# Routing in PSUM in a kernel of attention, mixture of experts, selective scan and mixing: one pair later, between two groups, with waits in another order

## The reference, cut to what matters

```python
h = _layernorm(x) * (1 + ca) + sa
x = x + ga * _L0_attn_ref(h, ...)        # 16 heads, grouped keys, relative positions
h = _layernorm(x) * (1 + cb) + sb
x = x + gb * _L0_ffn_ref(h, ...)         # mixture of 16 experts
...
x = x + ga * _L1_attn_ref(h, ...)        # selective scan, 256 channels x 16 states
x = x + gb * _L1_ffn_ref(h, ...)         # tanh of one product
```

```python
s = jax.nn.sigmoid(x2 @ Wg.T)
g = s.reshape(T, N_GROUPS, E // N_GROUPS)
_, gidx = jax.lax.top_k(g.max(axis=-1), TOPK_GROUPS)
group_mask = jnp.any(jax.nn.one_hot(gidx, N_GROUPS, dtype=jnp.bool_), axis=1)
masked = jnp.where(group_mask[:, :, None], g, -jnp.inf).reshape(T, E)
_, idx = jax.lax.top_k(masked, TOPK)
w = jnp.take_along_axis(s, idx, axis=1)
w = w / jnp.sum(w, axis=-1, keepdims=True) * ROUTE_SCALE
```

## Time and profile before

| | us |
|---|---|
| median of 3 runs | 2718.4 (2712.68 to 2719.95) |
| the profiled execution | 2723.16 |
| its span in the trace | 2721.4 |

### The profile page before, as it was taken

The page is one execution under the profiler, slowest core; times in us unless marked ns, Lnnn a source line. Parts: engine busy times, 40 slices in busy tenths (PEclk is TensorE's granted clock), DMA queues, the critical chain, the costliest instruction groups (busy, mean ns, idle before and its releaser), DMA issues.

```text
span 2721.4 us, 41804 instructions
## 1 busy us (share of the span) xinstructions
PE 2139.4 (79%) x11705; PEld 1002.0 (37%) x11840; DVE 1956.9 (72%) x3193; ACT 1624.3 (60%) x4159; POOL 1724.0 (63%) x2236
## 2 busy tenths in 40 slices
PE   4778988879798887878788887978888797877543
PEld 3344433434344333434343433434334343332110
DVE  2444658787786868777686868778587877778776
ACT  2655656666575666666566665757666566644442
POOL 1012258586776858577685857678585867777643
PEclk9889999999899999989899998989999899999665
DMA  7535395766667586665768676666857667454442
GB/s 141 90 61 102 58 177 109 148 129 143 122 112 156 104 158 127 147 125 117 136 120 166 121 133 126 127 130 124 164 109 146 127 140 129 97 127 128 118 117 69
DMA packets 534880, 338.84 MB, mean 125 GB/s; under 512 B 353929, under 2 KB 453177, under 8 KB 534201
## 3 DMA queue, kind: packets, MB, share of 16 engines
q1 hardware_dynamic: 534652, 336.16, 62.3%
HBM read 242.21 MB, written 26.74 MB: 99 GB/s over the span
## 4 chain that ended last, share of the span: by engine, by line
PE 30%; DVE 22%; POOL 16%; issue 14%; DMA 7%; ACT 7%; SPq 4%; POOLq 0%; ACTq 0%; DVEq 0%
DVE work L1241 6%; DMA bc<-bc_rows 5%; PE bank L623 5%; POOL work L1235 4%; POOL work L1248 4%; PE bank L909 3%; PE bank L954 3%; PE bank L651 3%; DVE nmax L631 3%; PE bank L1271 3%; POOL zh L967 2%; PE bank L972 2%; DVE step L1046 2%; PE bank L1072 2%; ACT probs L641 2%
## 5 line engine op out<-in xcount | busy, mean ns | idle before, releaser
L1235 POOL TENSOR_TENSOR work<-work,bc 128x512 f32<-128x512 f32 x512 | 658.5, 1292 | 188.7 <-PE bank L1271 132.7
L1241 DVE TENSOR_TENSOR_SCAN work<-bank,work 128x512 f32<-128x512 f32 x512 | 622.0, 1215 | 170.7 <-POOL work L1235 111.4
L1248 POOL TENSOR_TENSOR work<-work,bc 128x512 f32<-128x512 f32 x436 | 559.8, 1287 | 147.3 <-DVE work L1241 132.4
L967 POOL TENSOR_TENSOR zh<-zh,w_bc 128x512 f32<-128x512 f32 x256 | 326.9, 1277 | 403.4 <-DVE zh L960 403.1
L1224 ACT ACTIVATE bank<-work,neg_a 128x510 f32<-128x510 f32 x512 | 353.5, 691 | 370.1 <-DVE work L1241 349.5
L641 ACT ACTIVATE probs<-bank,nmax 128x256 f32<-128x256 f32 x1024 | 477.2, 479 | 69.2 <-DVE nmax L631 68.2
L631 DVE TENSOR_REDUCE nmax<-bank 128x2 f32<-128x512 f32 x512 | 336.0, 676 | 196.1 <-PE bank L623 195.9
L954 PE MATMUL bank<-h_b,w_t 128*128 128x512 f32 x512 | 293.7, 657 | 113.3 <-ACT probs L641 105.3
L651 PEld LDWEIGHTS bank<-ident,probs 128*128 128x128 f32 x2048 | 268.3, 151 | 293.8 <-issue 249.3
L659 ACT ACTIVATE probs_t<-bank 128x512 f32<-128x512 f32 x512 | 305.1, 596 | 106.6 <-PE bank L681 72.6
L623 PE MATMUL bank<-ke,q_all 64*64 64x256 f32 x4096 | 302.4, 413 | 84.4 <-DVE zh L960 47.8
(11 more groups left out here) (194 smaller groups left out, 2545.6 us busy)
## 6 DMA issues: line engine op xcount, KB each, us to landing
work<-dt_rows SPq DMA_DIRECT2D x256, 512.0 KB, 5.8
ke<-low SPq DMA_DIRECT2D x256, 256.0 KB, 5.8
w_bc<-w_rows_d SPq DMA_DIRECT2D x256, 256.0 KB, 5.1
q_all<-q_rows SPq DMA_DIRECT2D x1024, 8.0 KB
bc<-bc_rows SPq DMA_DIRECT2D x64, 256.0 KB, 8.4
x_in<-in_x SPq DMA_DIRECT2D x32, 256.0 KB, 5.5
dt_rows<-step SPq DMA_DIRECT2D x16, 512.0 KB, 3.5
dt_rows<-step SPq DMA_DIRECT2D x32, 256.0 KB, 2.5
```

Source lines behind the costliest of these rows:

```text
L967: nc.gpsimd.tensor_tensor(zh[:, n % 3, :], zh[:, n % 3, :], w_bc[:, n % WB, :], ALU.mult).then_inc(m_p, 1)
L1235: nc.gpsimd.tensor_tensor(hb[at % HB], ring[n % RING][:, 1, :], bc[:, s, :], ALU.mult).then_inc(s_dbx, 1)
L1241: nc.vector.tensor_tensor_scan(hb[at % HB], decay_bank(p, m)[:, :], hb[at % HB], 0.0, ALU.mult, ALU.add).then_inc(s_h, 1)
L1248: nc.gpsimd.tensor_tensor(hb[at % HB], hb[at % HB], bc[:, SG + batch(m)[2], :], ALU.mult).then_inc(s_hc, 1)
```

## The change

1. The results that the parts of the routing hand on lie in bank 3 of PSUM in turn with SBUF, so that no instruction has two inputs in SBUF. `route` cuts the bank. The group maximum is taken twice, into SBUF and into PSUM. The last two parts, times 0.5 * ROUTE_SCALE and times the score, become one; 20 parts are left.
2. They stand at steps 174 to 179 and not 167 to 178, behind the scaling of group 0 (step 173) of the next pair, for which part 0 waits (`groups_scaled`); the weights' transpose at 181 (178), its copy at 182 (179), the store at 183 (179), each expert's fetch one step earlier. The attention's statistics stand at -82 (-89), the last layernorm's at 512 (519). The last pair's routing keeps its steps but the last.
3. In seven functions the waits are listed in another order.

```diff
+        def route(lo, *shape):
+            ap = bank[3][:, lo:lo + math.prod(shape)]
...
-        equal = sb("equal", [P, TILES, NE])
-        top8 = sb("top8", [P, TILES, 8])
-        few = sb("few", [P, TILES])
-        ties = sb("ties", [P, TILES, NG, NG])
-        grank = sb("grank", [P, TILES, NG])
+        gate_p, ties_p, equal_p, picked_p = (route(64 * k, TILES, NE) for k in range(4))
+        ties = route(64, TILES, NG, NG)
+        gmax_p, open_p = (route(256 + 16 * k, TILES, NG) for k in range(2))
+        top8 = route(288, TILES, 8)
+        few = route(320, TILES)
...
-        ROUTE_STEPS, EXPERT, EVERY = 21, 192, 8
+        ROUTE_STEPS, EXPERT, EVERY = 20, 192, 8
...
-            68]], x_a_sync=-108, x_res_sync=104, a_store_sync=-33, m_store_sync=179,
-            m_fetch_sync=-8, s_rows_sync=376, s_rows_in_sync=[378, 391, 386, 380],
+            68]], x_a_sync=-108, x_res_sync=104, a_store_sync=-33, m_store_sync=183,
+            m_fetch_sync=-9, s_rows_sync=376, s_rows_in_sync=[378, 391, 386, 380],
...
-            m_route_vector=[167, 167, 167, 167, 169, 169, 169, 169, 170, 170, 170, 171, 172, 172,
-            173, 173, 174, 174, 174, 178, 178], m_end_vector=327, s_stats_vector=328,
+            m_route_vector=[174, 174, 174, 175, 175, 175, 175, 176, 176, 176, 177, 177, 177, 177, 178, 178, 178, 178, 179, 179], m_end_vector=327, s_stats_vector=328,
...
         def a_scores_tensor(pe, n, st):
             p, c = divmod(n, CHUNKS)
             b, x0 = c // (CHUNKS // 2), 2 * (c % (CHUNKS // 2))
+            if ups_before(st):
+                pe.wait_ge(m_b, ups_before(st))
+            if n:
+                pe.wait_ge(a_exp, n)
...
         def a_turn_tensor(pe, n):
-            pe.wait_ge(a_exp, n + 1)
             if n:
                 pe.wait_ge(a_tc, n)
+            pe.wait_ge(a_exp, n + 1)
...
         def a_turn_scalar(act, n):
-            act.wait_ge(a_t, n + 1)
             if n % CPG == 0 and n:
                 act.wait_ge(a_pv, n // CPG)
+            act.wait_ge(a_t, n + 1)
...
         def a_inverse_tensor(pe, n):
+            pe.wait_ge(a_ao, n + 1)
             pe.wait_ge(a_dg, n + 1)
-            pe.wait_ge(a_ao, n + 1)
...
-        def m_route_vector(dve, p, k):
+        def m_route_vector(dve, p, k, st):
             if k == 0:
                 dve.wait_ge(m_exp, p + 1)
+                if groups_scaled(st):
+                    dve.wait_ge(a_on, groups_scaled(st))
...
             elif k == 2:
-                nc.vector.tensor_reduce(gmax[:, :, :], score[:, :, :].rearrange("p t (g k) -> p t g k", g=NG), AX_X,
-                                        ALU.max).then_inc(m_ch, 1)
+                by_member = score[:, :, :].rearrange("p t (g k) -> p t g k", g=NG)
+                nc.vector.tensor_reduce(gmax[:, :, :], by_member, AX_X, ALU.max)
+                nc.vector.tensor_reduce(gmax_p, by_member, AX_X, ALU.max).then_inc(m_ch, 1)
             elif k == 3:
                 nc.vector.tensor_tensor(beats[:, :, :, :], other, own, ALU.is_gt)
-                nc.vector.tensor_tensor(ties[:, :, :, :], other, own, ALU.is_equal).then_inc(m_ch, 1)
+                nc.vector.tensor_tensor(ties, other, own, ALU.is_equal).then_inc(m_ch, 1)
...
             elif k == 15:
-                nc.vector.tensor_tensor(picked[:, :, :], picked[:, :, :], equal[:, :, :], ALU.add).then_inc(m_ch, 1)
+                nc.vector.tensor_tensor(picked_p, picked[:, :, :], equal_p, ALU.add).then_inc(m_ch, 1)
...
-            elif k == 19:
-                nc.vector.tensor_scalar(few[:, :], few[:, :], 0.5 * ROUTE_SCALE, None, ALU.mult).then_inc(m_ch, 1)
             else:
-                nc.vector.tensor_tensor(we[:, :, 0:NE], picked[:, :, :], few_e, ALU.mult).then_inc(m_ch, 1)
+                nc.vector.scalar_tensor_tensor(we[:, :, 0:NE], picked[:, :, :], 0.5 * ROUTE_SCALE, few_e, ALU.mult,
+                                               ALU.mult).then_inc(m_ch, 1)
...
         def m_gate_waits_tensor(pe, n):
 
+            if n:
+                pe.wait_ge(m_a, n)
...
-            act.wait_ge(s_in[n % RING], landed(p, n))
             if p >= FREE_PAIR and (p, m) != (FREE_PAIR, 0):
+                act.wait_ge(s_h, at - 1)
                 act.wait_ge(s_z1, 1)
-                act.wait_ge(s_h, at - 1)
             elif at:
                 act.wait_ge(s_h, at)
+            act.wait_ge(s_in[n % RING], landed(p, n))
...
         def s_input_gpsimd(pool, p, m):
             n, j, s = batch(m)
             at = BATCHES * p + m
+            if at >= HB:
+                pool.wait_ge(s_y, (at - HB) // 4 + 1)
+            pool.wait_ge(s_in[n % RING], landed(p, n))
             if m in (0, 4):
                 pool.wait_ge(bc_in[s], 16 * (p + 1))
```

More of the change, by code:

```diff
@@ L1 @@
 import itertools
+import math
 from contextlib import ExitStack
@@ L170, in build @@
         gz_t = [step[:, 2, :], step[:, 1, :]]
+        def route(lo, *shape):
+            ap = bank[3][:, lo:lo + math.prod(shape)]
+            if len(shape) == 1:
+                return ap
+            if len(shape) == 2:
+                return ap.rearrange("p (a b) -> p a b", b=shape[1])
+            return ap.rearrange("p (a b c) -> p a b c", b=shape[1], c=shape[2])
         gate = sb("gate", [P, TILES, NE])
@@ L444, in groups_valued, with groups_scaled @@
             return max(0, min(ALL_GROUPS, (st - 1 - AT["a_values_tensor"]) // GROUP_STEPS + 1))
+        def groups_scaled(st):
+            return max(0, min(ALL_GROUPS, (st - AT["a_scale_vector"]) // GROUP_STEPS + 1))
         def ln_stats_vector(dve, L, x, p):
@@ L787, in m_route_vector @@
             by_group = [P, TILES, NG, NG]
-            other, own = gmax[:, :, :].unsqueeze(2).broadcast_to(by_group), gmax[:, :, :].unsqueeze(3).broadcast_to(by_group)
+            other, own = gmax[:, :, :].unsqueeze(2).broadcast_to(by_group), gmax_p.unsqueeze(3).broadcast_to(by_group)
             flat_g, flat_e = "p t j i -> p t (j i)", "p t (g k) -> p (t g) k"
-            open_ = grank[:, :, :].rearrange("p t g -> p (t g)").unsqueeze(2).broadcast_to([P, TILES * NG, NE // NG])
+            open_ = open_p.rearrange("p t g -> p (t g)").unsqueeze(2).broadcast_to([P, TILES * NG, NE // NG])
@@ L791, in m_route_vector @@
             fourth = top8[:, :, TOPK - 1:TOPK].broadcast_to([P, TILES, NE])
[L792 removed]
+            few_e = few.unsqueeze(2).broadcast_to([P, TILES, NE])
             if k == 0:
[L795 removed]
+                nc.vector.tensor_scalar(gate_p, gate[:, :, :], 1.0, None, ALU.add).then_inc(m_ch, 1)
             elif k == 1:
[L797 removed]
+                nc.vector.reciprocal(score[:, :, :], gate_p).then_inc(m_ch, 1)
@@ L928, in m_gate_waits_tensor @@
                     pe.wait_ge(s_zg, 2 * ((n - GAP["z"][h]) // NE) + h + 1)
-            if n:
-                pe.wait_ge(m_a, n)
         def m_tanh_scalar(act, p, e):
@@ L1229, in s_input_gpsimd @@
             at = BATCHES * p + m
+            if at >= HB:
+                pool.wait_ge(s_y, (at - HB) // 4 + 1)
+            pool.wait_ge(s_in[n % RING], landed(p, n))
             if m in (0, 4):
                 pool.wait_ge(bc_in[s], 16 * (p + 1))
-            pool.wait_ge(s_in[n % RING], landed(p, n))
-            if at >= HB:
-                pool.wait_ge(s_y, (at - HB) // 4 + 1)
             nc.gpsimd.tensor_tensor(hb[at % HB], ring[n % RING][:, 1, :], bc[:, s, :], ALU.mult).then_inc(s_dbx, 1)
@@ L1623, in step_vector @@
                 if p is not None:
-                    m_route_vector(dve, p, k)
+                    m_route_vector(dve, p, k, st)
             p = due("m_end_vector", st)
```

47 lines of the change are left out of this document (20 added, 27 removed).

## The result

The median of five runs is 2692.7 us (2684.5 to 2703.1), beside 2717.8 us (2712.7 to 2720.0) for the kernel before: a ratio of 0.9913, 95% interval 0.9889 to 0.9938. That is 25 us off, where I forecast 43. Faster was right, the time lies in the range and 18 us above the forecast. The profiled execution has a span of 2694.6 us, against 2721.4.

The account below looks back on a forecast made before the run. VectorE's routing was taken to bound the stretch, its gain being how much earlier GpSimd gets on: 2.8 us x 13 pairs = 36, last pair 3, waits 4.5, together 43 off the median of 2718.4: 2675 us, range 2645 to 2711.

Parts of the forecast that it names:

- The stretched forms wait for GpSimd inside their own duration: VectorE's routing: nine long instructions wait on GpSimd over SBUF; PSUM operands shed 6.3 of 12.6 us a pair.
- VectorE's order set out anew: Routing stretch from 1036.8 us re-timed: root 1046.3, scan of step 52 ends 1056.7, GpSimd's instruction 1056.9 against 1059.73.
- ACT's 5.56 and PE's 4.58 us of idle time gone: Sign expected in the profile after: these single idle pieces of ACT and PE during the routing stretch disappear.
- Operand in PSUM: VectorE's small routing instructions: a PSUM operand costs nothing, bounded at 44 ns; at that bound 1.3 us over 30 instructions.
- PE's wait for the weights, and SyncE: Step 53 wait under 1 us, and fetch behind the weights' store 2 us: both hidden, taken at 0.
- Pairs 0 and 1 have no stretched forms, so nothing: First pairs: no stretched routing instructions there, so no gain was counted for them.
- Last pair: 3 us: Last pair's routing: four stretched instructions, some 4 us, of which 3 were put on the path.
- The rest of the pair is taken as it is: Steps outside the routing stretch were assumed unchanged; named the prediction's weakest step.
- Rival 2: Routing's operands in PSUM are dearer, +44 ns: 30 us off, 2688 us; chance 0.12.
- Rival 1: GpSimd's gaps in the routing stretch close wholly: 67 us off, 2651 us; chance 0.16.
- Rival 3: The new place takes back what the locks cost, at the root or PE's wait: 2710 us; chance 0.10.
- Rival 4: Slower: GpSimd's root waits for the moved statistics: +17 us, 2736 us; chance 0.08.

Follow-up runs that it names:

- experiment 1: Kernel after with the routing's intermediate results back in SBUF (one maximum), new steps and new waits kept: 2753.1 us, 1.0146 of the kernel before.
- experiments 1 and 2: The second of these: kernel after with one routing result, the sum of the two masks, back in SBUF: 2693.0 us, 0.9895 of the kernel before.
- experiment 5: Kernel after with the attention's statistics back at step 39 from 46: 2658.5 us; with four added matmuls 2651.4, with these and old waits 2658.0.
- experiment 4: Four unneeded matmuls a pair where PE waits in steps 8 to 15: kernel after 2674.2 us, kernel before 2704.5, kernel after with old waits 2675.5.
- PE busy: Matmuls that nobody needs, put where PE waits in steps 8 to 15: 2704.5 us on the kernel before, 2674.2 on the kernel after.

## Why the prediction was right, and where it was not

- *What bounds the kernel: VectorE in the routing, GpSimd's order behind it.* Right. Behind the stretch hardly anything moved (47.58 and 47.73 us), and GpSimd has the greatest part of the chain now.
- *The stretched forms wait for GpSimd inside their own duration, and one input in PSUM frees them.* Right: 12.7 to 6.5 us, against 6.3 us shed, and experiment 1 brings them back. The Trainium skill (SBUF — State Buffer, section SBUF: two separate sides) gives the reason: VectorE with two inputs in SBUF, or in a mode that uses two ports, and GpSimd take one pair of ports from each other for a whole instruction. By that rule the cost is set by GpSimd's instruction, and experiments 1 and 2 agree: 0.24 us beside GpSimd's instructions of 0.2 us, 1.05 to 1.19 beside those of 1.27, 0.36 at the end of one. Two inputs are not the whole of it: L795, with one, took 0.74 us, and with its output in PSUM (L808) 0.21.
- *VectorE's order set out anew.* Right, to within half a microsecond. GpSimd's input after its long gap starts at 1033.75 before and 1024.11 after, so 9.64 us are added to compare: root 1046.47 (forecast 1046.3), end of the scan of step 52 1056.26 (1056.7), GpSimd's read of step 55 1057.00 (1056.9).
- *ACT's 5.56 and PE's 4.58 us of idle time gone.* Wrong as a sign. They stand elsewhere: ACT idles 4.84 us before its decay at 1040.18, PE 4.81 before L986 at 1043.78. The weighing for which PE waits is queued behind the root, and the root behind the moved statistics. I had named that queue and looked only at whether VectorE waits for it. Experiment 5 shows its price: some 1.5 us a pair.
- *Operand in PSUM: nothing, at most 44 ns.* Nearly. The first part of the routing writes PSUM in 206 ns where the same instruction takes 160 into SBUF (experiment 1); all 30 together take 6.5 us where those of pair 0 before took 6.35. The 65 ns a read, an estimate worked out from the cycles that the Trainium skill gives (VectorE: DVE Perf Modes, section The TRN2 errata), are not seen: L820, which reads and writes PSUM, takes 0.23 us, and its like in SBUF 0.24 (L812 in experiment 1).
- *PE's wait for the weights, and SyncE: nothing.* Nothing was seen, but PE's 4.58 us, which were to cover the first, were not won. PE is itself late: its transposes of the weights (L871) follow its last matmul without a wait, 1.87 us after the routing's end in pair 7. The store of the weights goes at 1049.07, which with the 9.64 added is 1058.71; before, it went at 1058.64.
- *Waits, 4.5 us.* Right in size: 7.1, 4.5, 6.0 and 3.9 us in four pairings of traces. In the whole times it drowned.
- *13 pairs of 2.8 us.* The size was right, 2.73 a pair; with the waits the twelve ordinary pairs should have given 38 us and gave 37.1. The thirteenth, pair 15, gave 2.5, and 2.3 went in its steps 8 to 15.
- *Pairs 0 and 1 have no stretched forms, so nothing.* This step failed: 5.8 us lost in pairs 0 to 2. Steps 32 to 47 of pairs 1 and 2, at and just ahead of the new place, took 2.8 and 4.0 us more, and the rest of the three pairs 1 less; no stretched form was to be won there. The statistics are a part of it: with them back at step 39 these pairs take 316.8, 318.8, 317.9 and 319.7 us, in the seven kernels with them at step 46 318.6 to 325.5, at all the old steps 312.8 to 315.8. The rest, some 4 us, may be the routing in one piece; no run tried it alone.
- *Last pair: 3 us.* This failed too. Its routing sheds 4.0 us, but it was not what PE waited for. PE's transposes of the weights stand behind the turn of another layernorm, and that turn waits for ACT's normalisation in both kernels (first before, then after):

```profile
2457.38 1.09 PE L494 MATMUL bank<-ident,y_x 128*128 128x128 f32 x4 [11.35 <-ACT y_x L487]
2458.26 1.06 PE L857 MATMUL bank<-ident,we 128*32 128x128 f32 x4
```

```profile
2429.72 1.09 PE L505 MATMUL bank<-ident,y_x 128*128 128x128 f32 x4 [10.32 <-ACT y_x L498]
2430.60 1.06 PE L871 MATMUL bank<-ident,we 128*32 128x128 f32 x4
```

The routing ends 0.23 us before the transposes in the kernel before and 2.95 us before them in the kernel after: what it shed became a wait. Read from the traces, not tested by a run.

- *The rest of the pair is taken as it is*, which I had called the weakest step. It failed: 4.5 + 2.3 us went in steps 8 to 15. Experiment 4 shows that the 4.5 of the twelve ordinary pairs go when the low clock goes (0.6 are left); the 2.3 of pair 15 become 1.0 with PE busy (14.8 and 15.8 us), and where these come from is open. Nothing of PE's work there had changed.

Together 36 + 3 + 4.5 = 43 forecast, and found 37.1 + 2.5 in the pairs, less 5.8 in the head and 6.8 in steps 8 to 15, and the last 3 not had: 27. Three terms that I had put at nothing or at 3 us were off by 16 us together. The range had been made wide for other reasons, so that the time lies in it is partly luck. Rival 2 named 2688, near the time that came, for a reason that doesn't exist; a time that fits a rival is no evidence for it. Rival 1 (all gaps close) is what the kernel becomes when the statistics stay where they were: its 2651 is within 8 us of the 2658.5 of experiment 5. Rival 3 named 2710, and what it describes is there in part: by experiment 1 the new place costs 30 us in SBUF, and by experiment 5 its statistics cost 23 to 34 in PSUM. Rival 4 had the right mechanism, a root that waits for the statistics, at 1.6 us and not at 9.

## What to carry to other kernels

Where two engines hold each other up, price a part by what the other engine runs beside it, and move a part only with its queue in view: here PSUM gave 62 us at the new place, the new place cost 30 in SBUF, and leaving one small part of the move out gave 23 to 34 back. Look also at stages where the change wins nothing, since its price is paid there too. And before a few microseconds are put down to a change, look at the granted clock of TensorE in the stretches where PE waits: filling such waits with idle matmuls gave 18 us in one place and 26 in another, and a comparison that had come out at 25 us came out at 30, the sum of the rest of the trace, though the medians alone can't tell these apart.

## What the runs showed that I had not expected

Added matmuls of 3.6 us a pair made the kernel faster by 0.7%, because PE, after waits of 3.4 to 4.4 us in pairs 4 to 14 of the kernel after, went on at 1.2 GHz (L968 1.92 us in place of 1.02). How long the low clock lasted in these steps differed between pairs with the same work. The pairs' length follows it only loosely: in the kernel after, nine of the ten pairs 4 to 13 took 152.8 to 153.7 us, with 3.4 or 6.8 us of low clock in these steps, and one 157.0, with 10.2 and with steps 8 to 15 of 20.6 in place of 17.3 us. A change of a few microseconds elsewhere can so be covered: without PE busy the pairs of the kernel after are 3.3 us shorter than those before (153.6 and 156.9 in the middle), of which 2.7 are the routing's.
